# Attention in a fused transformer block: masks on the whole array, values of eight heads at once, score blocks regrouped

## The reference

```python
x = x + 0.5 * moe(layernorm(x))
x = x + attention(layernorm(x))      # this attention itself returns its input + out @ Wo
x = x + 0.5 * moe(layernorm(x))

q, k, v = x @ Wq, x @ Wk, x @ Wv     # 16 heads of 64
scores = q / 8 @ k.T, -inf above the diagonal
out = softmax(scores) @ v
```

## Time and profile before

| what | us |
|---|---|
| median of 3 timed runs | 1599.16 (1598.56 to 1599.58) |
| the profiled execution | 1598.77 |
| its span, first to last instruction | 1596.6 |
| PE busy | 1536.6 (96%) |
| DVE busy | 1184.4 (74%) |
| ACT busy | 786.6 (49%) |
| GpSimd busy | 332.4 (21%) |

### The profile page before, as it was taken

One profiled execution on the slowest core, in us unless ns is written; L12 is line 12 of the kernel. 1 busy time (PEld: TensorE's weight loads), 2 busy tenths in 40 slices (PEclk: granted clock), 3 DMA queues, 4 the chain that ended last, 5 costly groups with the idle time before them and its releaser, 6 DMA issues.

```text
span 1596.6 us, 29446 instructions
## 1 busy us (share of the span) xinstructions
PE 1536.6 (96%) x8768; PEld 1052.7 (66%) x8768; DVE 1184.4 (74%) x2797; ACT 786.6 (49%) x1856; POOL 332.4 (21%) x781
## 2 busy tenths in 40 slices
PE   2999999999989999999999999999979999999998
PEld 2666666666666666666666666667646666666665
DVE  6977787777767677777767677777768777877775
ACT  3344333342466656566666666666643443333422
POOL 2000000000144444444444444444320000000000
PEclk9999999999999999999999999999999999999999
DMA  6443333333200000000000000000003333333342
GB/s 189 130 154 103 113 103 103 114 108 114 67 1 1 1 1 1 0 0 0 0 0 0 0 0 0 0 0 1 1 21 115 115 103 119 114 112 116 105 121 86
DMA packets 58802, 97.16 MB, mean 61 GB/s; under 512 B 6144, under 2 KB 15360, under 8 KB 58752
## 3 DMA queue, kind: packets, MB, share of 16 engines
q1 hardware_dynamic: 58752, 96.53, 19.8%
HBM read 92.83 MB, written 3.67 MB: 60 GB/s over the span
## 4 chain that ended last, share of the span: by engine, by line
PE 47%; issue 29%; POOL 19%; DVE 4%; DMA 1%; POOLq 1%; ACT 0%; SPq 0%; DVEq 0%
PE banks L375 17%; POOL work L1281 16%; PE banks L199 9%; PE banks L201 9%; PE banks L200 9%; POOL pool_pace L1276 3%; PE banks L337 1%; PE banks L347 1%; DVE work L1060 1%; DVE work L1032 1%; POOLq L1275 0%; DMA bias<-in_gate_bias 0%; DVE bn L870 0%; DMA work<-cw_rows 0%; DVE chosen L980 0%
## 5 line engine op out<-in xcount | busy, mean ns | idle before, releaser
L692 ACT ACTIVATE work<-banks 128x512 f32<-128x512 f32 x336 | 200.7, 598 | 462.7 <-PE banks L201 443.6
L1032 DVE TENSOR_TENSOR work<-banks,work 128x512 f32<-128x512 f32 x336 | 231.9, 690 | 153.1 <-ACT work L692 148.0
L375 PE MATMUL banks<-work,wd 128*128 128x512 f32 x672 | 342.8, 593 | 0.3 <-DVE work L1060 0.3
L749 ACT ACTIVATE work<-banks,nmax 128x512 f32<-128x512 f32 (+3 forms) x512 | 264.5, 530 | 73.9 <-DVE nmax L1114 71.9
L1281 POOL TENSOR_SCALAR work<-work,rrec 128x512 f32<-128x512 f32 (+3 forms) x512 | 269.0, 538 | 1.6
L199 PE MATMUL banks<-xT_hi,wg_hi 128*128 (+1 forms) x336 | 248.4, 739 | 0.0
L1060 DVE TENSOR_TENSOR work<-work 128x512 f32<-128x512 f32 x320 | 226.0, 706 | 15.9 <-DVE work L1032 9.3
L489 PE MATMUL banks<-small,work 128*128 128x128 f32 x1280 | 200.8, 280 | 11.8 <-POOL work L1281 6.0
L1114 DVE TENSOR_REDUCE nmax<-banks 128x2 f32<-128x1024 f32 (+3 forms) x256 | 203.3, 816 | 3.2 <-PE banks L478 3.2
L489 PEld LDWEIGHTS banks<-small,work 128*128 128x128 f32 x1280 | 146.4, 141 | 52.4 <-issue 14.9
L1132 DVE COPY stage<-banks 128x512 f32<-128x512 f32 x256 | 174.9, 684 | 0.9 <-PE banks L489 0.9
(11 more groups left out here) (121 smaller groups left out, 2285.3 us busy)
## 6 DMA issues: line engine op xcount, KB each, us to landing
work<-cw_rows SPq DMA_DIRECT2D x320, 256.0 KB, 3.2
x<-in_x SPq DMA_DIRECT2D x8, 256.0 KB, 7.8
out_rows<-x SPq DMA_DIRECT2D x8, 256.0 KB, 2.4
cw_rows<-cwT SPq DMA_DIRECT2D x16, 96.0 KB, 2.0
stage<-in_w_gate SPq DMA_DIRECT2D x3, 448.0 KB, 6.0
stage<-in_w_up SPq DMA_DIRECT2D x3, 448.0 KB, 6.7
wd<-in_w_down SPq DMA_DIRECT2D x3, 448.0 KB, 7.9
small<-in_small SPq DMA_DIRECT2D x1, 576.0 KB, 4.0
```

What stands on the lines that cost most here:

```text
L375: pe.matmul(psY, wd[:, j * P:(j + 1) * P], z[part_slot(j)], start=j == 0, stop=j == HT - 1, skip_group_check=True).then_inc(s["down_ps"], 1)
L692: nc.scalar.activation(silu[j % 2], psG[j % 3], ACT.Silu) \
L749: m = nc.scalar.activation(prob[:, p % 2, i, o:o + w], ps[:, i, so:so + w], ACT.Exp, bias=nmax[:, p % 2, i, qb:qb + 1], accum_out=rsum[:, ...
L1032: tt(gated[j % 3], psU[j % 3], silu[j % 2], ALU.mult) \
```

## The change

Masks: a mask matmul now comes first in its bank, once per head, with the whole 128x128 identity and the full mask, and the scores are added to it. The masks of score blocks 0 and 1 stand at the head of the slot, then the scores of blocks 0 and 1; the masks and scores of block 2 stand directly ahead of the weighted sum, which now comes before the transposes of parts 3 and 4.

Values: one three-pass product gives the values of eight heads (512 columns) for one tile of 128 rows. A batch needs eight of these, one for each slot, three slots ahead. They are kept in two buffers, of heads 0 to 7 and 8 to 15. `wv` is split into high and low like the other weights; `xT_whole` goes.

DVE takes the maximum of block 1 directly behind that of block 0. ACT copies part 3 behind the exponentials of block 2. The next batch's rows are prepared one slot earlier. The constants are smaller: the masks are no longer stored in halves, and iota is no longer repeated 6 times. The batch loop on PE is unrolled by two.

```diff
-SMALL = 7 * P + E * TOPK + TB * G * G
+SMALL = 2 * P + E + TB * G * G
...
-            def project_values(b, p):
-                for t in range(TB):
-                    m = pe.matmul(psC[:, t * P:(t + 1) * P], xT_whole[:, t * P:(t + 1) * P],
-                                  wv[:, p * P:(p + 1) * P], start=True, stop=True,
-                                  skip_group_check=True)
-                m.then_inc(s["v_ps"], 1)
-            def scores(b, p, u, first):
+            def project_values(parity, k):
+                t, i = k % TB, k // TB
+                rows = slice(parity * CH + t * P, parity * CH + (t + 1) * P)
+                mm3(pe, psC, [x[:, rows] for x in xT_parts],
+                    [w[:, 3, i * CH:(i + 1) * CH] for w in aw], True, True).then_inc(s["v_ps"], 1)
+            def masks(b, p, u, first):
+                n = pair(b, p)
+                if not (first and p == 0 and u < 2):
+                    pe.wait_ge(s["exp_done"], 4 * n + (-2, 0, 1)[u])
+                o, w = ((3 * P, P), (2 * P, P), (P, 2 * P))[u]
+                for i in (0, 1):
+                    pe.matmul(score_banks(p, u)[:, i, o:o + w], ident_bf, mask_bf[:, 0:w], start=True,
+                              stop=False, skip_group_check=True)
+            def scores(b, p, u):
...
-                o, w = ((3 * P, P), (2 * P, P), (P, 2 * P))[u]
-                for k in (0, 1):
-                    for i in (0, 1):
-                        r = slice(i * DK, (i + 1) * DK)
-                        m = pe.matmul(ps[:, i, o:o + w], half[r, k * P:(k + 1) * P],
-                                      half[r, 2 * (k + 1) * P:2 * (k + 1) * P + w], start=False,
-                                      stop=k == 1, skip_group_check=True)
...
             def attn_slot(b, p, parity, first, last):          # PE
...
                 if have_s:
-                    scores(*ahead(b, p, 1), 0, False)
+                    masks(*ahead(b, p, 1), 0, False)
+                    masks(*ahead(b, p, 1), 1, False)
+                    scores(*ahead(b, p, 1), 0)
+                    scores(*ahead(b, p, 1), 1)
...
                 probT(b, p, 0)
-                if have_s:
-                    scores(*ahead(b, p, 1), 1, False)
...
                 probT(b, p, 2)
+                if have_v:
+                    wait_pT(1, n)
+                    if p == 5:
+                        pe.wait_ge(s["a_xT_lo"], b + 2)
+                    project_values((parity + (p >= 5)) % 2, (p + 3) % HP)
                 if have_s:
-                    scores(*ahead(b, p, 1), 2, False)
-                if have_q:
+                    masks(*ahead(b, p, 1), 2, False)
+                    scores(*ahead(b, p, 1), 2)
+                if p == 4 and not last:
+                    pe.wait_ge(s["v_sb"], n + 4)
+                    a_prep(b + 1, psC)
...
+                if not (first and p == 0):
+                    wait_pT(2, n)
+                    attend(*ahead(b, p, -1))
...
                 probT(b, p, 3)
-                if p == 5 and not last:
-                    pe.wait_ge(s["v_sb"], n + 3)
-                    a_prep(b + 1, psC)
-                if not (first and p == 0):
-                    wait_pT(2, n)
-                    attend(*ahead(b, p, -1))
...
             def attention():                                    # PE
...
-                pe.wait_ge(s["v_sb"], 1)
-                project_values(0, 1)
+                for k in (1, 2):
+                    pe.wait_ge(s["v_sb"], k)
+                    project_values(0, k)
...
             def a_xT_high(b, ps):                               # ACT
-                nc.scalar.activation(xT_whole[:, :], ps, ACT.Copy)
...
             def attn_slot(b, p, first, last):                   # ACT
...
-                if have_q:
-                    value_copy(*ahead(b, p, 2), first and p < 2)
-                for part in PT_ACT:
-                    pT_copy(b, p, part, first and p < 2)
-                if p == 5 and not last:
+                if not (last and p >= 5):
+                    value_copy(*ahead(b, p, 3), first and p < 5)
+                if p == 4 and not last:
                     a_xT_high(b + 1, psC)
...
                 if have_s:
                     exp(*ahead(b, p, 1), 2, False)
+                for part in PT_ACT:
+                    pT_copy(b, p, part, first and p < 2)
...
             def attn_slot(b, p, first, last):                   # DVE
...
                 if have_s:
                     row_max(*ahead(b, p, 1), 0)
+                    row_max(*ahead(b, p, 1), 1)
                 if have_q:
                     part_lo(*ahead(b, p, 2), 0, False)
                 pT_copy(b, p, 0, first and p < 2)
                 if have_s:
                     row_rec(*ahead(b, p, 1), 0)
-                    row_max(*ahead(b, p, 1), 1)
...
-                if p in (2, 3) and not last:
-                    a_rows(b + 1, False, (2 * (p - 2), 2 * (p - 2) + 1))
-                if p == 4 and not last:
+                if p in (1, 2) and not last:
+                    a_rows(b + 1, False, (2 * (p - 1), 2 * (p - 1) + 1))
+                if p == 3 and not last:
                     a_residual(b + 1)
                 if have_s:
                     row_max(*ahead(b, p, 1), 2)
-                if p == 5 and not last:
+                if p == 4 and not last:
                     a_xT_low(b + 1, psC)
...
-            nc.vector.tensor_copy(half[:, :], small[:, P:7 * P])
+            nc.vector.tensor_copy(half[:, 0:2 * P], small[:, 0:2 * P])
+            nc.vector.tensor_copy(half[:, 2 * P:], small[:, P:2 * P])
...
-            for w in range(3):
+            for w in range(4):                                  # GpSimd, weight splits
```

More of the change, by code:

```diff
@@ L114, in build @@
         prob = work[:, 0:4 * PW].rearrange("p (r i c) -> p r i c", r=2, i=2)
-        NV = 4
-        values = work[:, 10 * CH:].rearrange("p (k t d) -> p k t d", k=NV, t=TB)
+        values = [work[:, 10 * CH:].rearrange("p (t d) -> p t d", t=TB),
+                  sb("values", [P, TB, CH])[:, :, :]]
         x = sb("x", [P, NT, P])
@@ L430, in ffn @@
                 if g0 == 0:
-                    scores(0, 0, 0, True)
-                    scores(0, 0, 1, True)
+                    masks(0, 0, 0, True)
+                    masks(0, 0, 1, True)
+                    scores(0, 0, 0)
+                    scores(0, 0, 1)
                 pe.wait_ge(s["x_added"], g0 + NC - 1)
@@ L461, in scores @@
                     pe.wait_ge(s["k_lo"], n + 1)
-                if not (first and p == 0 and u < 2):
-                    pe.wait_ge(s["exp_done"], 4 * n + (-2, 0, 1)[u])
                 ps = score_banks(p, u)
@@ L505, in attend @@
                         o = i * PW + KB_OFF[kb]
-                        m = pe.matmul(psB[i * DK:(i + 1) * DK, kb * P:], values[:, p % NV, kb, i * DK:(i + 1) * DK],
+                        m = pe.matmul(psB[i * DK:(i + 1) * DK, kb * P:], values[p // TB][:, kb, p % TB * P + i * DK:p % TB * P + (i + 1) * DK],
                                       pT[:, p % 2, o:o + w], start=kb == 0, stop=kb == TB - 1,
@@ L523, in rows_out, with attn_slot @@
                 to_columns(psO, outT[:, :].rearrange("p (t d) -> p t d", t=TB)).then_inc(s["outT_ps"], 1)
-            def attn_slot(b, p, first, last):
+            def attn_slot(b, p, parity, first, last):
                 n = pair(b, p)
+                have_v = not (last and p >= 5)
                 have_s = not (last and p + 1 >= HP)
@@ L728, in part_hi, with value_copy @@
                     .then_inc(s[("q_hi", "k_hi")[which]], 1)
-            def value_copy(b, p, early):
-                n = pair(b, p)
-                act.wait_ge(s["v_ps"], n + 1)
-                if not early:
-                    act.wait_ge(s["ctx_ps"], n - 3)
-                nc.scalar.activation(values[:, p % NV, :, :].rearrange("p t d -> p (t d)"), psC, ACT.Copy) \
+            def value_copy(b, k, first):
+                act.wait_ge(s["v_ps"], b * HP + k + 1)
+                if k % TB == 0 and not first:
+                    act.wait_ge(s["ctx_ps"], b * HP + k - TB)
+                nc.scalar.activation(values[k // TB][:, k % TB, :], psC, ACT.Copy) \
                     .then_inc(s["v_sb"], 1)
@@ L973, in route_onehot @@
                 dve.wait_ge(s["route"], g * ROUTE + 28)
-                step(tt(onehot[:, :, :, :], iota.unsqueeze(1).broadcast_to([P, TB, E, TOPK]),
+                step(tt(onehot[:, :, :, :], iota.unsqueeze(1).unsqueeze(3).broadcast_to([P, TB, E, TOPK]),
                         topf[:, :, 0:TOPK].unsqueeze(2).broadcast_to([P, TB, E, TOPK]),
```

68 lines of the change are left out of this document (33 added, 35 removed).

## The result

| | us |
|---|---|
| changed kernel, median of 4 runs | 1648.08 (1642.81 to 1651.7) |
| kernel before, median of 4 runs | 1598.86 (1597.87 to 1599.58) |
| ratio, with its 95% interval | 1.0303 (1.029 to 1.0317) |
| forecast | 1641 (1620 to 1660) |
| the profiled execution after, and its span | 1648.04, 1646.0 |

The change costs 49 us. PE has 15.7 us less to do than before, yet the span grew by 49.4.

A forecast was written before the change was run, and what follows sets the result against it. Ring B (11.99 us) was to bound plain slots, Ring A (11.54) slots 1 to 4: 4 x 11.99 + 4 x 11.54 + 4.2 = 98.3 a batch against 92.2. 1598.8 + 43 + 0.7 - 1.5 = 1641 us, range 1620 to 1660.

The forecast's parts named there:

- The rings: Closed chains of in-order waits through PE, DVE and ACT; two were summed, 11.99 and 11.54 us a slot.
- Ring B: Plain slots: q's low part, k projection, block 1's exponentials, copy of part 2, weighted sum, part 3, ctx, maxima; 11.99 us.
- Ring A: Slots 1 to 4 of a batch: the chain through block 2's exponentials instead of block 1 to weighted sum; 11.54 us.
- once-per-batch work: Work done once a batch in slots 1 to 4: 3.0 us on DVE and 1.2 on ACT, 4.2 together.
- PE's sum: PE's own work in a plain slot: 11.18 us less 0.79 (three form changes 0.60, values 0.19), so 10.39.
- the prediction's own sign: Check on the array-form step: right if PE's busy time in a plain slot falls to 10.2 to 10.6 us.
- PE stays the bound: Rival: chains of waits close below 10.39 us, every slot gains 0.79, 1548 us; 5 in 100.
- Ring B doesn't close: Rival: part 2's copy is ready before the weighted sum asks, so Ring A alone sets all slots, 1628 us; 16 in 100.
- Level: Rival: something counted on both chains of waits is hidden, 0.8 us a slot, so 1599 us; 4 in 100.
- The clock falls: Rival: PE's waits drop its clock to 1.2 GHz over a tenth of the slots, 25 us more, 1666; 5 in 100.

The follow-up runs named there:

- experiment 1: Changed kernel with, on DVE, the reciprocal of block 1 moved behind the copy of transposed part 2: 1625.54 us.
- experiment 2: Changed kernel with, on ACT, the copy of transposed part 3 moved behind ctx_hi of the next slot: 1610.21 us.
- experiment 3: Changed kernel with block 1's reciprocal behind the copy of part 2 (DVE) and the copy of part 3 behind ctx_hi (ACT): 1590.55 us.
- experiment 4: Changed kernel with the maximum of block 1 put back behind the reciprocal of block 0 on DVE: 1648.64 us.
- experiment 7: Changed kernel with DVE's order rewritten and the copy of part 3 behind ctx_hi on ACT: 1566.48 us.
- experiment 6: Changed kernel with DVE's order rewritten so that copies freeing a bank go ahead of what waits for ACT: 1574.94 us.
- experiment 8: Kernel before the change with only its PE batch loop unrolled by two, 16 slots a pass: 1603.29 us.
- experiment 5: Changed kernel with the weighted sum back between parts 3 and 4 and the copy of part 3 back ahead of block 2's exponentials: 1612.44 us.

## Why the prediction was right

**The rings.** Right in place and nearly in size. Ring B was summed to 11.99 and measured 11.78. Its step of 0.13 from DVE to PE was mis-sized: both crossings took 0.05, which is 0.16 of the 0.21; the transposes of part 3 with their crossing took 0.69 and not 0.74, the other 0.05. The other steps agree to 0.02. That the exponentials, the copy of part 3 and the reciprocal bind is shown by experiments 1 to 3, not only read off. Four plain slots were to take 47.96 and took 47.4; slots 1 to 4 were to take 50.4 and took 50.64. That is 98.1 a batch, forecast 98.3. Ring A, summed to 11.54, is under ring B by ACT's idle time ahead of the copy of part 3: 11.78 - 0.37 = 11.41. So the closeness of slots 1 to 4 is partly luck: four times 11.41 leaves 5.0 for the once-per-batch work, where 4.2 was forecast, and ring A's 0.13 a slot too much made up for most of it. What I had missed are more rings of nearly the same length: experiment 1 met one at 11.41, experiment 4 one at 11.94. They didn't change the forecast, but they would have made a forecast of any single undoing wrong. Which ring holds the 11.10 of experiment 2 I didn't sum.

**PE's sum.** Wrong in size: 10.39 forecast, 10.67 measured (experiment 7), so 0.51 saved and not 0.79. By the prediction's own sign (busy time of 10.2 to 10.6) this step failed. Three products are dearer: values 0.81 where I had put 0.70 (+0.11), k 0.80 (+0.10), output 0.86 (+0.07). Together 0.28, which is the miss.

The values stand behind fp32 transposes, and their first pass takes 0.34 there, not 0.23. That is a cost on PE that I mis-sized. The other 0.17 is the wait of experiment 7. Before, the weights of the k projection were loaded ahead of time, 0.22 us before its first pass, and its passes followed at 0.23:

```profile
805.87 0.19 PEld L199 LDWEIGHTS banks<-xT_hi,aw_hi 128*128 128x128 f32 x1
806.09 0.39 PE L199 MATMUL banks<-xT_hi,aw_hi 128*128 x1
806.32 0.39 PE L200 MATMUL banks<-xT_lo,aw_hi 128*128 x1
```

In experiment 7 q's low part ends at 782.67, so that the load and the first pass both start at 782.72 and the second pass only at 783.06:

```profile
782.72 0.50 PE L196 MATMUL banks<-xT_hi,aw_hi 128*128 128x512 f32 x1
783.06 0.39 PE L197 MATMUL banks<-xT_lo,aw_hi 128*128 128x512 f32 x1
```

Without that wait PE's sum would be about 10.5, an estimate from these rows (10.67 - 0.17); no run tries it. For the time of the changed kernel none of this mattered, since the rings bind.

**PE stays the bound, 1548.** False for this order, as experiments 1 to 3 and 6 show by opening the rings. With rings A and B open and no loop turns, 1559 is reached, not 1548: the rival's 0.79 a slot was too much.

**Ring B doesn't close, 1628.** False, by PE's 0.30 ahead of the weighted sum, and by experiment 1, which opens ring B and gets 1625.54 (it takes the exponentials of block 1 out of ring A too, so it isn't quite this rival's case).

**Level, 1599**, needed 0.8 hidden from both rings; nothing was.

**The clock falls, 1666.** Not over the five batches shown: PE is idle for 50 of 493 us, and the granted clock is 1.00.

**The balance.** The forecast was 42 us over before; the spans differ by 49.4. The six middle batches were to cost 37 and cost 38.2, 2.5 of it the two loop turns, which I had put at nothing. At the start DVE begins 0.8 us earlier, where 1.5 was forecast. That the smaller constants do it isn't shown: before and after, its first instruction waits for the load of `in_gate_bias`, and in the runs with the smaller constants it begins anywhere from 5.90 to 8.42 us, against 7.14 before. The scores of the first slot stand 1.2 us later, where 0.8 less was forecast. The first and last batch together cost 8.0, where I counted one batch of 6.1. And 2.0 us lie behind the last scores; their cause stays open. Over all the runs that stretch takes 428.4 to 434.0 us, so 2.0 is within what it scatters. These small terms, each 1 to 3 us, are the 7 us between 1641 and 1648.

## What to carry to other kernels

An engine that is full hides the rings of waits behind it. Before making it faster, sum each ring (one bank or buffer, its owners in order, and every in-order neighbour that stands ahead of an owner's wait); the new time is at least the longest of the engine's sum and these, and a ring that nobody summed can make it longer (here by up to 0.2 us a slot). On the engines beside the bound, put what frees a bank ahead of what waits for another engine: the same instructions in another order were worth 73 us of 1648 here, while undoing one move alone was worth nothing. An engine that is busy for the whole of a stretch can still be waiting there, if the end of one matmul hides the gap before the next. And a loop body made longer had a price at its turns, the largest where the engine that loops was the bound.

## What the runs showed of the hardware

- A PE loop body of 16 slots costs a wait for issue at each turn: 1.4 to 1.9 us in the changed kernel and in experiment 8, 2.33 to 4.16 in experiments 6 and 7, where PE is the bound; a body of 8 slots and straight code had none between 520 and 1140 us.
- Behind the 4.16 us wait the granted clock was 0.57 for 4 us; behind the 1.4 us wait at the changed kernel's first turn it stayed at 1.00. Over the loop turns of the changed kernel and of experiments 1 to 8, it stayed at 1.00 behind all waits of 1.40 to 1.91 us; of the waits of 2.0 us and more it stayed so behind two (2.45 us each, experiments 4 and 5) and was 0.50 to 0.63 for 4 us behind the other eight.
- From the end of a DVE instruction to the matmul that it releases took 0.05 us in ring B, and 0.13 in the earlier trace rows.
- A three-pass product's first pass takes 0.34 and not 0.23 behind fp32 transposes, within the whole-array form as well (832.50 to 832.84), and also where a wait held its weight load back (782.72 to 783.06).
